# Expert rows kept in DRAM as fp16 halves and turned by DMA transposes

## The reference

```python
x = x + tanh(g_xattn[0]) * xattn(layernorm(x), ctx, ctx, Wq, bq, ..., Wo, bo)
x = x + tanh(g_ffn[0]) * ffn(layernorm(x), ...)
# in ffn, with E, CAP, C, H = 64, 512, 1024, 128
shared = silu(g_s) * y_s @ w_shared_down
scores = sigmoid(x_flat @ w_gate); _, topk_idx = top_k(scores, 6)
x_disp = zeros((E, CAP, C)).at[flat_e, pos].set(x_flat[token_ids], mode='drop')
up = einsum('ecd,edh->ech', x_disp, w_up)          # per expert 512x1024 by 1024x256
g_r, v_r = split(up, 2)
out_r = einsum('ech,ehd->ecd', silu(g_r) * v_r, w_down)   # 512x128 by 128x1024
routed = (out_r gathered back * w).sum over the 6
```

## Time and profile before

| | |
|---|---|
| median of 3 runs | 3170.62 us (3170.16 to 3171.55) |
| the profiled execution | 3170.95 us, of which span 3169.2 us |
| mean granted clock of TensorE | 0.977 of full speed |
| PE busy | 2986.0 us (94%) |
| DVE, ACT, POOL busy | 2214.7, 1346.0, 1372.6 us |
| DMA moved | 546.48 MB, mean 172 GB/s |
| q1, share of 16 engines over the span | 309.12 MB, 32.0% |
| q0, share of 16 engines over the span | 235.06 MB, 31.7% |

### The profile page before, as it was taken

How to read it: one execution, slowest core, us unless ns; L and a number is a source line. 1 busy time by engine, 2 the same in 40 slices (tenths; PEclk the granted TensorE clock), 3 DMA queues, 4 the chain that set the end, 5 groups by cost and what they waited for, 6 DMA issues and landing times. The chain is left out here.

```text
span 3169.2 us, 62918 instructions
## 1 busy us (share of the span) xinstructions
PE 2986.0 (94%) x21248; PEld 1813.3 (57%) x21248; DVE 2214.7 (70%) x3818; ACT 1346.0 (42%) x2172; POOL 1372.6 (43%) x1316
## 2 busy tenths in 40 slices
PE   5899999999999994999999969999999999999996
PEld 4677777777777762444444425555555555555552
DVE  6677777777777776777777755666666666666663
ACT  4444444444444442111111105555555555555552
POOL 1222222222222212445555544666666666666663
PEclk9999999999999996999999989999999999999998
DMA  7333334333333335444444427999999999999996
GB/s 235 78 88 84 88 88 107 98 85 87 85 87 85 87 97 177 123 140 139 134 139 133 138 80 217 269 282 278 265 275 276 264 281 280 278 286 270 284 273 138
DMA packets 433545, 546.48 MB, mean 172 GB/s; under 512 B 230391, under 2 KB 328695, under 8 KB 433376
## 3 DMA queue, kind: packets, MB, share of 16 engines
q1 hardware_dynamic: 353504, 309.12, 32.0%
q0 software_dynamic: 79872, 235.06, 31.7%
HBM read 340.27 MB, written 203.88 MB: 172 GB/s over the span
## 5 line engine op out<-in xcount | busy, mean ns | idle before, releaser
L1559 POOL DMA_INDIRECT out<-outs,target x256 | 402.3, 1572 | 296.2 <-ACT outs L1636 237.0
L1657 DVE TENSOR_TENSOR ext_lo<-eturn_ps,ext_hi 128x1024 f16<-128x1024 f32 x254 | 311.1, 1225 | 266.3 <-ACT ext_hi L1606 258.6
L1530 POOL DMA_INDIRECT rows<-rows_dram,index x256 | 355.2, 1388 | 120.7 <-POOL index L1526 59.4
L1606 ACT ACTIVATE ext_hi<-eturn_ps 128x1024 f16<-128x1024 f32 x254 | 260.1, 1024 | 220.6 <-PE eturn_ps L1720 164.1
L733 PE MATMUL proj_ps<-xt,wq_wo_hi 128*128 128x256 f16 x1024 | 280.5, 274 | 28.0 <-DMA xt<-xw 27.3
L1720 PE MATMUL eturn_ps<-ident,rows 128*128 128x128 f32 x2032 | 268.4, 275 | 28.5 <-DMA rows<-rows_dram,index 24.4
L733 PE MATMUL proj_ps<-ct_hi,wk_wv_hi 128*128 128x256 f16 x1024 | 280.2, 274 | 8.0 <-issue 8.0
L734 PE MATMUL proj_ps<-xt,wq_wo_hi 128*128 128x256 f16 x1024 | 280.3, 274 | 1.1 <-issue 1.1
L1720 PEld LDWEIGHTS eturn_ps<-ident,rows 128*128 128x128 f32 x2032 | 224.5, 141 | 97.6 <-DVE ext_lo L1657 50.1
L735 PE MATMUL proj_ps<-xt,wq_wo_lo 128*128 128x256 f16 x1024 | 280.2, 274 | 0.0
L734 PE MATMUL proj_ps<-ct_lo,wk_wv_hi 128*128 128x256 f16 x1024 | 280.0, 273 | 0.0
(11 more groups left out here) (179 smaller groups left out, 7307.5 us busy)
## 6 DMA issues: line engine op xcount, KB each, us to landing
ew_in<-w_up SPq DMA_DIRECT2D x64, 1024.0 KB
ew_in<-w_down SPq DMA_DIRECT2D x64, 512.0 KB
x_in<-x SPq DMA_DIRECT2D x16, 1024.0 KB, 5.7
c_in<-ctx_t SPq DMA_DIRECT2D x16, 1024.0 KB, 7.9
v_dram<-vt SPq DMA_DIRECT2D x64, 256.0 KB, 2.0
late<-v_dram SPq DMA_DIRECT2D x32, 512.0 KB, 8.3
attn_dram<-attn SPq DMA_DIRECT2D x64, 256.0 KB, 2.0
a_in<-attn_dram SPq DMA_DIRECT2D x32, 512.0 KB, 4.0
```

What stands on the lines that cost most here:

```text
L1530: pool.indirect_dma_start(out=rows[:, par * TPE + k, :], out_offset=None, in_=rows_dram, in_offset=bass.IndirectOffsetOnAxis(ap=index[:, p ...
L1559: pool.indirect_dma_start(out=out, out_offset=bass.IndirectOffsetOnAxis(ap=target[:, k:k + 1], axis=0), in_=outs[:, k, :], in_offset=None, ...
L1606: act.activation(xt_hi[:, e.base % 2, :, k * P:(k + 1) * P], turned_ps(e, k), ACT.Copy).then_inc(xt_hi_made, 1)
L1657: dve.tensor_tensor(xt_lo[:, e.base % 2, :, cols], turned_ps(e, k), xt_hi[:, e.base % 2, :, cols], ALU.subtract).then_inc(xt_lo_made, 1)
```

## The change

The normalised rows are no longer stored in `rows_dram` as fp32, but as the two fp16 halves side by side (2 x 1024 fp16, again 4 KB a row). The store now reads `yw`, stands behind the wait for the low half, and ahead of the same DMA transpose to `yt` as before. The guard of `rows_stored` moves from DVE's write of `yn` to ACT's write of `yw`.

In the expert stage the gather brings both halves at once. SP then issues, for each tile, a DMA transpose of the 128 x 2048 fp16 from `rows` into `xt`, which holds both halves (`ext` in the trace); it stands in SP's order ahead of the loads of weights. PE's fp32 transposes, ACT's copy and DVE's subtraction are gone, as is `eturn_ps`. PE waits for the four transposes of an expert (`turned`) ahead of its matmuls.

```diff
@@ routing stage, SP @@
-                        sp.wait_ge(y_normed, s.times(1, 1))
-                        sp.sem_inc(apart, 1)
-                        sp.dma_start(rows_dram[bass.ds(s.times(P), P), :], yn[:, s.base % 2]
-                                     ).then_inc(rows_stored[s.base % 2], 16)
-
                         sp.wait_ge(y_lo_made, s.times(1, 1))
                         sp.sem_inc(apart, 1)
+                        sp.dma_start(rows_dram[bass.ds(s.times(P), P), :],
+                                     yw[:, s.base % 2].rearrange("p w d -> p (w d)")
+                                     ).then_inc(rows_stored[s.base % 2], 16)
...
@@ ACT, ahead of the high half @@
                         act.wait_ge(y_turned, t.times(16, -16))
+                        act.wait_ge(rows_stored[t.base % 2], t.half().times(16))
...
@@ DVE, norm @@
-                    dve.wait_ge(rows_stored[par], t.half().times(16))
...
@@ expert stage, tensors @@
-        rows = sb("rows", [P, 2 * TPE, D], F32)
+        rows = sb("rows", [P, 2 * TPE, 2 * D], F16)
-        xt_hi = sb("ext_hi", [P, 2, KC, CAP], F16)
-        xt_lo = sb("ext_lo", [P, 2, KC, CAP], F16)
+        xt = sb("ext", [P, 2, 2, KC, CAP], F16)
-        turn_ps = ps("eturn_ps", [P, KC, P])
...
@@ SP @@
+                def turn(e, k):
+                    par = e.base % 2
+                    sp.wait_ge(gathered[par][k], e.half().times(16, 16))
+                    sp.sem_inc(apart, 1)
+                    if k == 0:
+
+                        sp.wait_ge(v_made, e.times(1, -1))
+                        sp.sem_inc(apart, 1)
+                    sp.dma_start_transpose(xt[:, par, :, :, k * P:(k + 1) * P].rearrange("p w c t -> p (w c) t"),
+                                           rows[:, par * TPE + k, :]).then_inc(turned[par][k], 16)
+
                 def first():
                     ...
                     load_w(Step(0))
-
                     for k in range(TPE):
-                        sp.wait_ge(gathered[0][k], 16)
+                        turn(Step(0), k)
                     load_w(Step(1))
 
                 def step(e, up, down):
+                    if up and more(e, 1):
+                        for k in range(TPE):
+                            turn(e.plus(1), k)
                     if more(e, 2):
                         load_w(e.plus(2))
...
@@ POOL, gather @@
-                    pool.wait_ge(turned, e.times(TPE, -TPE))
-                    pool.sem_inc(apart, 1)
+                    for k in range(TPE):
+                        pool.wait_ge(turned[par][k], e.half().times(16))
+                        pool.sem_inc(apart, 1)
...
@@ ACT; DVE's turn with its subtraction goes in the same way @@
-                def turn(e, k):
-                    act.wait_ge(turned, e.times(TPE, k + 1))
-                    if k == 0:
-
-                        act.wait_ge(v_made, e.times(1, -1))
-                    act.activation(xt_hi[:, e.base % 2, :, k * P:(k + 1) * P], turned_ps(e, k), ACT.Copy
-                                   ).then_inc(xt_hi_made, 1)
...
@@ PE @@
-                def turn(e, k):
-                    ...
-                    pe.wait_ge(xt_lo_made, max(k - 1, 0) if first else e.times(TPE, k))
-                    for c in range(KC):
-                        last = pe.transpose(turned_ps(e, k)[:, c, :], rows[:, par * TPE + k, c * P:(c + 1) * P], ident[:])
-                    last.then_inc(turned, 1)
-
...
-                        pe.matmul(out, wh, xt_hi[:, par, c, :], start=(c == 0), stop=False)
-                        pe.matmul(out, wh, xt_lo[:, par, c, :], start=False, stop=False)
-                        last = pe.matmul(out, wl, xt_hi[:, par, c, :], start=False, stop=(c == KC - 1))
+                        pe.matmul(out, wh, xt[:, par, 0, c, :], start=(c == 0), stop=False)
+                        pe.matmul(out, wh, xt[:, par, 1, c, :], start=False, stop=False)
+                        last = pe.matmul(out, wl, xt[:, par, 0, c, :], start=False, stop=(c == KC - 1))
...
                         pe.wait_ge(w_lo_made[UP], e.times(1, 1))
-                        pe.wait_ge(xt_lo_made, e.times(TPE, TPE))
+                        for k in range(TPE):
+                            pe.wait_ge(turned[e.base % 2][k], e.half().times(16, 16))
...
-                                if more(e, 1):
-                                    turn(e.plus(1), 2 * part + half)
                                 up_half(e, part, half)
```

More of the change, by code:

```diff
@@ L1436, in expert_phase @@
         down_ps = [ps(f"edown_ps{i}", [P, D]) for i in range(2)]
-        spare_turn_ps = down_ps[1][:].rearrange("p (k t) -> p k t", k=KC)
         table_landed = sem("table_landed")
@@ L1451, in expert_phase @@
         w_lo_made = [sem(f"w_lo_made{part}") for part in (UP, DOWN)]
-        turned = sem("turned")
-        xt_hi_made = sem("xt_hi_made")
-        xt_lo_made = sem("xt_lo_made")
+        turned = [[sem(f"turned{i}_{k}") for k in range(TPE)] for i in range(2)]
         g_made = sem("g_made")
@@ L1465, in expert_phase @@
         rows_added = [sem(f"rows_added{k}") for k in range(TPE)]
-        def turned_ps(e, k):
-            return spare_turn_ps if e.register is None and e.base == 0 and k % 2 else turn_ps[:]
         def more(e, ahead):
@@ L1599, in split_h @@
                     act.activation(h_hi[:, e.base % 2, :], hidden[:], ACT.Copy).then_inc(h_hi_made, 1)
-                def turn(e, k):
-                    act.wait_ge(turned, e.times(TPE, k + 1))
-                    if k == 0:
-                        act.wait_ge(v_made, e.times(1, -1))
-                    act.activation(xt_hi[:, e.base % 2, :, k * P:(k + 1) * P], turned_ps(e, k), ACT.Copy
-                                   ).then_inc(xt_hi_made, 1)
                 def first():
                     split_w(Step(0), UP)
-                    for k in range(TPE):
-                        turn(Step(0), k)
                 def step(e, up, down):
@@ L1616, in step @@
                     for k in range(TPE):
-                        if up and more(e, 1):
-                            turn(e.plus(1), k)
                         if k == 0 and more(e, 1):
@@ L1748, in first @@
                 def first():
-                    for k in range(TPE):
-                        turn(Step(0), k)
+                    pass
                 def step(e, up, down):
@@ L1776, in gated_cross_attention_and_moe @@
     attn_dram = nc.dram_tensor("attn_dram", [NBLK * NP * P, 2 * KC * SQ], F32, kind="Internal").ap()
-    rows_dram = nc.dram_tensor("rows_dram", [N, D], F32, kind="Internal").ap()
+    rows_dram = nc.dram_tensor("rows_dram", [N, 2 * D], F16, kind="Internal").ap()
     table_dram = nc.dram_tensor("table_dram", [E * CAP, 2], F32, kind="Internal").ap()
```

## The result

The changed kernel takes 3978.95 us (median of 4 runs, 3916.3 to 4059.53) against 3171.09 us before: a ratio of 1.242 (95% interval 1.234 to 1.250). The runs of one and the same program lie 143 us apart, where those of the kernel before lie 2 us apart; that is part of the finding. The traced execution is the slowest of them, 4059.53 us, and its figures for each expert are some 1.7 us above those of the faster runs, from which the ratio comes. It gives 31.5 us an expert for the changed kernel, where I forecast 29.1.

What follows compares the result with a forecast made beforehand. PE sets the pace at 19.08 us an expert, with the DMA engines nearly full. 61 experts pay 10.0 us for transposes, plus 10 us of start, less 4 us at the end: 3787 us, range 3620 to 4030.

Steps and rivals of the forecast that it cites:

- the DMA engines had no room: Expert stage: transfers without transposes need 18.3 of 19.08 us an expert, leaving at most 0.7 us to spare.
- PE's gain of 3.5 us: Expert stage: PE loses four turns, 3.5 us an expert, and would need 15.6 us.
- the routing stage: Store moved ahead of the transpose to yt: zero, except 2 us in the last tile; the moved guard: zero.
- the start: Start of the expert stage: longer memset and expert 0's transposes ahead of the first matmul, taken as 10 us.
- rival A: Expert stage: PE is cold as well, 31 to 33 us an expert, 3900 to 4020 us; chance 0.16.
- step 3: Expert stage: four added DMA transposes of 2.5 us each add to the other transfers, 10.0 us an expert.
- B: Expert stage: each transpose keeps other traffic off until landed, 4.3 us each, 4220 us; chance 0.05.
- C: Expert stage: a transpose costs only its bytes at the gather rate, 1.34 us, total 3500 us; chance 0.12.
- D: Expert stage: transposes vanish under the accumulates, period 18.3 us an expert, total 3128 us; chance 0.03.
- the DMA share had no holes: Expert stage sign: DMA share still near 1.04 to 1.1; holes would mean step 3 is wrong.
- the equal places: Expert stage sign: equal places two experts apart recur after about 58 us.
- PE's wait: Expert stage sign: PE's first matmul of g_ps waits some 10 us or more for the DMA transposes.

Runs made afterwards that it cites:

- e1: The changed kernel with the rows of experts 2 to 63 not turned at all: 3145.6 us, ratio 0.992.
- e7: The changed kernel with transposes waiting for the accumulates and POOL's transfers waiting for the transposes: 4186.6 us, ratio 1.321.
- e8: The changed kernel without accumulates, gathers for experts 0 and 1 only, each transpose issued twice: 3378.7 us, ratio 1.065.
- e2: The changed kernel without the accumulates to out and their waits: 3417.5 us, ratio 1.079.
- e4: The changed kernel with two of the four tiles of an expert turned from expert 2 on: 3721.6 us, ratio 1.173.
- e3: The changed kernel with gathers for experts 0 and 1 only, later transposes turning those rows again: 3649.3 us, ratio 1.139.
- e11: The changed kernel without accumulates, gathers also waiting until the transposes in flight have landed: 3171.3 us, ratio to the kernel before 1.0005.
- e6: The changed kernel with 16 instead of 48 matmuls for g_ps and v_ps: 4069.4 us, ratio 1.282.
- e10: The changed kernel without turns from expert 2 on and with accumulates that skip the empty slots: 3129.4 us, ratio 0.984.
- e5: The changed kernel, overlapped, with accumulates that skip the empty row slots: 3958.2 us, ratio 1.235.
- e12: The phased kernel e7 with accumulates that skip the empty row slots: 4032.1 us.

## Why the prediction held, and where it did not

The direction, the place and the cause of the first 8 us were right: the DMA engines had no room, e1 measures 18.5 us for 18.3 (with the ring of `outs` as near), PE's gain of 3.5 us was worth nothing, and the routing stage and the start cost what was said (8.5 us for 10). From 80 to 1000 us PE is busy 888.7 us in the changed kernel and 889.4 before, and from 1500 to 1850 us all of the time in both.

The forecast of 3787 us was 192 us short of the median, inside the range of 3620 to 4030 and outside its own narrower one of 3700 to 3880. That the wide range reached so far up was for rival A, a cold PE, which is not what happened: that part of the hit is luck. The step that failed is step 3, "So they add". Its price and its sum were both off, in opposite ways, and one of its two readings was wrong:

- The price of a transpose. I took 2.5 us from one that runs alone, where filling and draining count. Four in a row take 8.0 us, 2.0 each, 261 GB/s (e7), and in e8 2.3 us with weights between. Here the Trainium skill, DMA: Bandwidth & Descriptors (Latency and other measured facts), with its 261 GB/s was nearer than my row; the phased trace, at 261 GB/s in its window, agrees. By e7's price alone the period would be 18.3 + 8.0 = 26.3 us.
- The mixture. I read the earlier trace rows, one microsecond in which accumulates and weights meet at 175 GB/s, as proof that the queues don't help each other, and stopped there; it was also a sign that they can harm each other. Measured, the overlapped loop takes 31.5 us for 26.3 us of work, 5.2 us an expert, 317 us in all. The same excess is 7.1 us in e2 (23.0 against 7.9 + 8.0), 5.6 in e4, 3.8 in e3, and 3.0 us with all hand-overs in e11, where transposes meet gathers less. Why it is larger without accumulates (e2) than with them stays open.
- The reading of the earlier trace rows. I took the silence of the weights' queue in that microsecond as the two queues keeping each other off. But the expert stage's first load, issued at 1889.17 us with nothing on POOL's queue, also moves its first packet 1.6 us later, behind the table's, so most of that microsecond is the load's own start. From 2005 to 2006 us loads and gathers run side by side at full rate:

```profile
DMA packets 314, 0.40 MB, mean 399 GB/s; under 512 B 11, under 2 KB 285, under 8 KB 314
...
q1 hardware_dynamic: 274, 0.28, 78.8%
q0 software_dynamic: 40, 0.12, 29.4%
```

The bytes still add, but plain loads beside gathers do no harm; the excess comes with the transposes (e1, without them, has none).

Of the rivals, A (a cold PE) had the right range, 3900 to 4020 us, for the wrong reason: e6 made PE shorter and the kernel slower. The granted clock did fall to 0.77, but PE's wait of 16 us an expert covers it. B, 4.3 us a transpose through landings, is refuted by e7 and e8. C, cheap transposes, is wrong for the kernel, and for a transpose by itself as well: 2.0 us lies between its 1.34 and my 2.5, nearer to mine. D, hidden under the accumulates, is the reverse of what e3 shows.

Of what I said would show: the DMA share had no holes, the equal places lie 66 us apart in the traced execution where I had 58, and PE's wait is 16 us where I had 10 or more. The rate in phases without POOL's transfers was above, not near, 210 GB/s.

The long SP instructions (45.6% of the span in the chain) are an effect: SP issues four transposes in 7.8 us when nothing is beside them. Read by itself, the chain would have blamed SP.

What stays open is the mechanism of the stall in the DMA engines: the traces show packets of both queues open at once at a rate of 48 to 67 GB/s, not what they wait for. Whether the transpose's small packets (2080 for 0.52 MB) or the turning itself does it was not tried. Nor did I try one tile in four turned by DMA beside skipped empty slots; e4, where two tiles cost 8.8 us against 1.7 us saved on PE, speaks against it.

## What to carry to other kernels

Before work moves from an engine to DMA, add up the bytes of a period at the rates that each kind has alone; if the sum is the period already, as here, the move costs its full price, however idle the engine becomes. Read DMA share and rate together: the share alone says little (four transposes alone have 1.18 at 261 GB/s), but 1.46 at 67 GB/s is transfers that disturb each other. Then keeping two kinds apart with a wait can be faster than overlap (e2 to e11, 246 us); keeping all of them apart was not (e7, 208 us slower than the changed kernel). Runs of one program that scatter by several per cent, when the old ones agreed to 0.1%, are a reason to look for it, though not a proof: e10, without transposes, scatters by 52 us too.

## What the hardware showed that I had not expected

- Transposes beside indirect DMAs of the other queue: 48 to 89 GB/s together for microseconds at a time, where transposes alone move 261 to 285 and gathers 303.
- A quarter fewer bytes of accumulates gained nothing measurable in the mixture (e5) and 154.5 us in phases (e12).
- A lone transpose of 128 x 2048 fp16 fills the engines 2.5 us, each of four in a row 2.0 (e7).
- Leaving out two thirds of the matmuls of `g_ps` and `v_ps` made the kernel 3% slower (e6).
